# Cross attention on one core: scores of token tiles 2 and 3 issued together in the third block of a quarter

## What is computed

```python
x = x + xattn(layernorm(x), ctx, ctx, Wq, bq, Wk, bk, Wv, bv, Wo, bo)
# x is (2, 2048, 512), ctx is (2, 154, 512), 16 heads of 32
scores = einsum('bhqd,bhkd->bhqk', q, k) / sqrt(32)
attn = softmax(scores); out = einsum('bhqk,bhkd->bhqd', attn, v) @ Wo.T + bo
x = x + ffn(layernorm(x))
```

## Time and profile before

| what | value |
| --- | --- |
| median of 3 runs (range) | 3585.88 us (3585.81 to 3586.5) |
| the profiled execution: its own time, its span | 3587.36 us, 3585.6 us |
| PE, DVE, ACT, POOL busy, share of the span | 96%, 63%, 42%, 32% |
| mean granted clock of PE | 0.987 |

### The profile page before, as it was taken

One profiled execution on the slowest core, in us unless ns is written; L12 is line 12 of the kernel. 1 busy time (PEld: TensorE's weight loads), 2 busy tenths in 40 slices (PEclk: granted clock), 3 DMA queues, 4 the chain that ended last, 5 costly groups with the idle time before them and its releaser, 6 DMA issues. The chain is left out here.

```text
span 3585.6 us, 56360 instructions
## 1 busy us (share of the span) xinstructions
PE 3447.5 (96%) x20560; PEld 2795.2 (78%) x20560; DVE 2271.9 (63%) x4996; ACT 1500.6 (42%) x3978; POOL 1138.8 (32%) x1008
## 2 busy tenths in 40 slices
PE   7999996999999989999999989999999899999999
PEld 5676675888888877888888868888888678888887
DVE  6888875999999984222322259999999642333322
ACT  5666663555555543111111145555555421111111
POOL 3434433555555520000000045555555121101111
PEclk9999998999999999999999989999999999999999
DMA  4112213111121122111111121112111331111111
GB/s 123 42 45 64 71 42 124 57 55 58 61 68 60 57 73 88 44 44 43 42 43 44 64 75 57 57 55 75 57 59 53 97 111 40 46 49 49 40 41 38
DMA packets 186869, 216.26 MB, mean 60 GB/s; under 512 B 27094, under 2 KB 125654, under 8 KB 186595
## 3 DMA queue, kind: packets, MB, share of 16 engines
q1 hardware_dynamic: 186595, 212.65, 18.5%
HBM read 125.79 MB, written 69.00 MB: 54 GB/s over the span
## 5 line engine op out<-in xcount | busy, mean ns | idle before, releaser
L1893 DVE SCALAR_TENSOR_TENSOR u_full<-banks,b_cols,gate 128x512 f32<-128x512 f32 (+1 forms) x176 | 132.1, 751 | 875.4 <-ACT gate L1851 802.4
L46 PE MATMUL banks<-fxT_h,w_h 128*128 128x512 f32 (+1 forms) x1408 | 556.3, 395 | 3.0 <-DVE w_l L1877 2.6
L48 PE MATMUL banks<-fxT_h,w_l 128*128 128x512 f32 (+1 forms) x1408 | 556.1, 395 | 0.0
L47 PE MATMUL banks<-fxT_l,w_h 128*128 128x512 f32 (+1 forms) x1408 | 555.2, 394 | 0.0
L1851 ACT ACTIVATE gate<-banks,b_cols 128x512 f32<-128x512 f32 (+1 forms) x176 | 121.2, 689 | 1007.1 <-PE banks L48 1007.1
L1746 POOL TENSOR_TENSOR sums<-sums,b_rows 128x512 f32<-128x512 f32 x64 | 85.2, 1363 | 877.6 <-DMA sums<-z_rows 877.6
L1146 POOL TENSOR_TENSOR rn<-ssq,neg_half 128x8 f32<-128x8 f32 x128 | 210.8, 1647 | 412.3 <-DVE ssq L1419 405.9
L46 PE MATMUL banks<-wqkv_h,hT_h 128*128 128x512 f32 x768 | 324.9, 423 | 15.0 <-DVE wqkv_l L1406 15.0
L1355 ACT ACTIVATE pT_h<-banks 128x384 fp32r<-128x384 f32 (+2 forms) x512 | 213.9, 470 | 257.5 <-PE banks L1244 256.5
L1460 DVE TENSOR_SCALAR prob<-prob,rc 128x384 f32<-128x384 f32 (+2 forms) x512 | 313.5, 654 | 9.1
L46 PEld LDWEIGHTS banks<-fxT_h,w_h 128*128 128x128 f32 (+1 forms) x1408 | 259.6, 184 | 72.0 <-DVE w_l L1877 4.3
(11 more groups left out here) (190 smaller groups left out, 8183.2 us busy)
## 6 DMA issues: line engine op xcount, KB each, us to landing
y_rows<-sums SPq DMA_DIRECT2D x16, 1024.0 KB
sums<-y_rows SPq DMA_DIRECT2D x64, 256.0 KB, 3.0
z_rows<-sums SPq DMA_DIRECT2D x64, 256.0 KB, 2.0
sums<-z_rows SPq DMA_DIRECT2D x16, 1024.0 KB, 5.8
thirds<-in_w SPq DMA_DIRECT2D x30, 512.0 KB, 4.8
thirds<-in_x SPq DMA_DIRECT2D x8, 1024.0 KB, 6.8
x_rows<-thirds SPq DMA_DIRECT2D x8, 1024.0 KB, 4.3
thirds<-y_rows SPq DMA_DIRECT2D x64, 128.0 KB, 2.8
```

What stands on the lines that cost most here:

```text
L46: pe.matmul(out, a_h, b_h, start=start, stop=False)
L47: pe.matmul(out, a_h, b_l, start=False, stop=False)
L48: return pe.matmul(out, a_l, b_h, start=False, stop=stop)
L1893: e.scalar_tensor_tensor(out=u_full[r, m % 2, :], in0=ps[r, 2 * (m % 2), :], scalar=b1[r, place[m], 0:1], in1=gate[r, :], op0=ALU.add, op1 ...
```

## The change

Nothing is computed otherwise. In the 31 quarters in which scores of a next quarter are made:

- PE: `scores` of tile 2 leaves block 1 and stands in block 2, directly in front of `scores` of tile 3.
- ACT: `exps` of tile 2 goes from block 1 to block 2, and `exps` of tile 3 from block 2 to block 3, behind `hi_q` and `hi_p` of that block.
- DVE: `maxima` of tile 2 goes from block 1 to block 2. `maxima` of tile 3 stays in block 2 but goes behind `lo_p`. `recip` of tiles 2 and 3 goes from blocks 2 and 3 to blocks 3 and 4.
- POOL: its code is unchanged, but its divisions of tiles 2 and 3 wait for those reciprocals.

```diff
 PE
-                            if k < GT - 1 and not (g.last and q == DC - 1):
-                                scores(it, q + 1, k + 1)
+                            if k in (0, 2) and not (g.last and q == DC - 1):
+                                scores(it, q + 1, k + 1 if k == 0 else k)
+                                if k == 2:
+                                    scores(it, q + 1, 3)
                             transpose_p(it, m, g.last)
 ACT
-                            if k < GT - 1 and more:
-                                exps(it, q + 1, k + 1)
+                            if k in (0, 2, 3) and more:
+                                exps(it, q + 1, max(k, 1))
 DVE
-                            if k < GT - 1 and more:
-                                maxima(it, q + 1, k + 1)
+                            if k in (0, 2) and more:
+                                maxima(it, q + 1, max(k, 1))
                             if k == 1 and (q or old):
                                 lo_o(it, q - 1)
-                            if k < GT and more:
-                                recip(it, q + 1, k)
+                            if k in (0, 1, 3, 4) and more:
+                                recip(it, q + 1, (0, 1, None, 2, 3)[k])
                             lo_p(it, QK * q + k, 4 + (QK * q + k if g.last else turn(q, k, 0)) % 2)
                             if (q, k) in X_SLOT and not g.last:
                                 lo_x(it + 1, X_SLOT[q, k], 4 + turn(q, k, 1) % 2)
+                            if k == 2 and more:
+                                maxima(it, q + 1, 3)
```

## The result

The changed kernel took 3595.70 us (median of 11 runs, 3592.57 to 3599.87), the kernel before, run beside it, 3587.37 us (11 runs, 3585.81 to 3589.21). The ratio is 1.0023 with a 95% interval of 1.0014 to 1.0033: 8.3 us slower, where 9.1 had been forecast. That is clear of noise; whether it is more than the 0.2% (7.2 us) at which the prediction counts a change as one is not settled by this interval.

A forecast was written before the change was run, and what follows sets the result against it. Chains through ACT and DVE were taken to set the time around PE's waits, PE only the stretches between. Terms 11.3 - 4.5 + 0.65 + 1.65 = +9.1 us on 3585.9 gave 3595.0 us; range 3586 to 3602, including the cancelling case.

The forecast's parts named there:

- PE's drain, 0.3 us a pair: On PE, merging two groups of scores spares a tiling-mode drain, 0.3 us in each of 31 quarters.
- The list of PE's waits: Seven recurring PE waits per group before the change, four naming DVE, two ACT, one POOL, adding to 4.81 us.
- Quarter 2, +0.72: Exponents of tile 3 push `hi_p` of block 4 on ACT, so the next quarter's first `maxima` starts 0.72 us late.
- Quarter 3, +0.89: Exponents of tile 3 delay `hi_p` of block 4; the next `maxima` is 1.61 us late, 0.89 more than at quarter start.
- The hold of 1.25 us: In quarter 3 POOL's bias addition holds DVE's negative of the maxima, 1.25 us for some 0.17; forecast to meet tile 2.
- Quarter 0, nothing: DVE's chain to `lo_q` has no gap, so the 1.61 us lateness is carried unchanged to the projection.
- Quarter 1, -0.75: `lo_q` starts 0.76 us earlier and the transposes of block 4 leave 0.75 us earlier.
- both parts of it: Quarter 1: `hi_q` behind tile 2's exponents only, and two `finish` at 1.00 us for 1.53 without a division beside them.
- Sum: Middle group 0.72 + 0.89 - 0.75 = +0.86 us; whole phase 11.3 - 4.5 + 0.65 + 1.65 = +9.1 us.
- 1.61 - 0.3 + 1.95: 1.61: quarters 2 and 3 of a group; +1.95: last group's extra; 0.3: PE regains in that group's quarter 0.
- PE is the bound: Faster rival: PE bounds throughout, each merge saves its drain, -9.3 us in all, 3576.6; chance 0.13.
- Much slower by the stalls: Rival: late divisions stall PE in block 0 by 0.84 and 2.17 us, quarter 1 regains nothing; +21, 3607; chance 0.10.

The follow-up runs named there:

- the one-quarter runs: Four kernels, each with the new order in only one of quarters 0, 1, 2, 3: periods 64.88, 64.09, 65.63, 65.88 us against 64.90 in the kernel before.
- the quarter alone: New order only in quarter 2, old order in the others: period 65.63 us against 64.90 in the kernel before.
- quarter 0 alone: New order only in quarter 0, old order in the others: period 64.88 us against 64.90 in the kernel before.
- The kernel with the exponents back in front: Changed kernel with exponents of tile 3 back in block 2, directly behind those of tile 2: period 68.26 us against 65.74.
- quarter 3 alone: New order only in quarter 3, old order in the others: period 65.88 us against 64.90 in the kernel before, groups with clock falls left out.
- short division: Changed kernel, last division of quarters 2 and 3 cut to one head of four: 65.76 us in one stretch without clock falls, later 68.1 to 68.2.
- quarter 1 alone with the moved additions: New order only in quarter 1, POOL's bias additions moved: to quarters 1 and 2, 3586.49 us; all behind quarter 0, 3581.92 us; which one is not said.

## Why the prediction was right, step by step

- *PE's drain, 0.3 us a pair:* the scores together do run closer, but the one-quarter runs show no gain from it in quarters 0, 2 and 3, and the gain of quarter 1 has another source. In quarter 0 it ended as idle time. The list of PE's waits in the prediction was one short: the wait of 0.36 for exponents in quarter 0 (311.49) is missing, so there were eight and 5.17 us of them. It changed no term, since that time too went into the wait for the queries.
- *Quarter 2, +0.72:* measured 0.72 on DVE, 0.71 on PE, and 0.73 for the quarter alone. The forecast of two waits at unchanged ends held (1.10 and 0.82, forecast 1.3 and 0.8), as did the wait for POOL in block 0 of quarter 3, 0.78, and the single wait for exponents, 1.10 for 1.3.
- *Quarter 3, +0.89:* measured 0.95 to 0.98. The hold of 1.25 us was where I had put it; taking it away is worth 0.66 us a group (65.74 - 65.08). The transposes of quarter 0 started 2.06 late, where I had 2.17, but PE's wait for POOL in front of them was 1.01 and not over 2: PE itself came 1.3 late to it (314.10 - 1.01 - 2.97 = 310.12, before 309.07 - 0.25 = 308.82), which I had not followed.
- *Quarter 0, nothing:* the projection came 1.67 late for 1.61, and quarter 0 alone gave -0.02.
- *Quarter 1, -0.75:* measured -0.83, and -0.81 alone. `finish` at 1.00 and the wait of 0.62 (forecast 0.7) show that both parts of it came. They cannot be priced apart. In the kernel before `hi_q` (the row below, timeline of ACT before) ended at 342.47 and the two `finish` at 342.36, and `lo_q` followed at 342.50. By these rows an earlier `hi_q` alone would have given some 0.2 us at most and a shorter `finish` alone nothing; that is an estimate. The kernel with the exponents back in front had the short `finish` (1.00) with a `hi_q` that was later still; there `lo_q` waited 1.32 for `hi_q`, and the quarter gained nothing.

```profile
341.77 0.70 ACT L759 ACTIVATE xqT_h<-banks,bq_cols 128x512 fp32r<-128x512 f32 x1
```

- *Sum:* +0.84 a group for +0.86, and +8.3 between the medians for +9.1. In the traces the phase itself is 8.91 longer, but part of that closeness is luck, since two misses cancel. Up to block 4 of quarter 1 in the first group the loss is 0.53, where I had +0.65, with one fall of the clock in it (73 to 77 us) that the kernel before does not have. From the same row in the seventh group to the end of the phase it is 2.6, where my terms give 1.61 - 0.3 + 1.95 = 3.3. The six periods between add to 5.75 and not to the 5.16 forecast, since three of them are longer than 65.76 (66.04, 65.90 and 65.97), two of these by a fall of the clock, for which the prediction had no term. The chances do not add up as written either: with a quarter of 0.55 below 7.2 us they come to 0.51, 0.36 and 0.13 and not to 0.53, 0.32 and 0.15.
- *The rivals:* "PE is the bound" is out by the one-quarter runs. "Much slower by the stalls" is not what the changed kernel does, but its mechanism appears as soon as the divisions get another 0.9 us later.

## What to carry to other kernels

When work is moved one block later in an in-order queue, what it costs is decided by the next instruction behind it, and who waits for that: here four exponents of 1.46 us were free in one quarter, won 0.8 in another where they had stood in front of something urgent (and a division moved out of the way with them), and lost 0.7 and 1.0 where they came to stand in front of the high part of block 4. A pattern that repeats need not have one answer for all its repeats, so such a change should be tried for each of them alone. And a merge that closes gaps on the fullest engine gives nothing if the time is set by a chain through the others; look at which wait ends last.

## What the runs showed of the hardware that I had not expected

PE's granted clock fell behind some of its longer waits. In the changed kernel (windows of PE: busy us, granted clock, DMA), behind a wait of 1.01 us that ended at 182.46:

```profile
178.00:182.00 4.00, 3.14 (x22) 1.00 0.00 0
182.00:186.00 4.00, 3.54 (x11) 0.57 0.01 4
186.00:190.00 4.00, 4.00 (x27) 1.00 0.00 0
```

The transposes there took 1.09 us for four in place of 0.66, and matmuls of 512 columns 0.63 in place of 0.39, for some 3 us. Behind the equal wait at 314.10 nothing of the kind happened. The kernel before has no such fall between 90 and 545 us; its waits there reach 1.18. Between the same times the changed kernel has two in its profiled execution, quarter 0 alone has one and quarter 3 alone four, three of these behind waits of 1.17 and 1.18 that the kernel before has too. The kernels with waits of 1.43 (exponents back) and 1.27 with 1.90 (short division) have one in every group and, from the third group on, two in every group. So the length of the wait in front does not settle it, and what does no run here shows. One fall costs PE 1.4 to 1.6 us: from the transposes at 182.46 to those two blocks later it is 7.84, and 6.28 behind 314.10. How much of it reaches the end of the group depends on where it comes: 0.16 in the changed kernel (a period of 65.90 in place of 65.74), where the wait for the queries in front of the projection took up the rest, and all of 1.4 with quarter 3 alone (67.26 for 65.88), where it came in quarter 2. This fits the wider scatter of the changed kernel, 7.3 us from the fastest to the slowest run for 3.4 of the kernel before, and over its 11 runs the slowest has a mean granted clock of 0.984 and the two fastest 0.987. But quarter 1 alone with the moved additions scatters by 7.9 us, also with the lower clocks (0.984 and 0.985) in its slowest runs, while its trace has no fall between 90 and 545 us. A trace exists only of one run of each, so falls of this kind as the cause of the scatter are argued, not shown.

The holds were the other point. An instruction of four columns on DVE, 0.17 us when nothing is in its way, took 1.25 us beside an addition on POOL (303.40 before, 306.91 changed) and another one 1.14 (344.92), each until the addition was over. The Trainium skill (SBUF — State Buffer, SBUF: two separate sides) states that a VectorE instruction in a 2-port mode and a GpSimd instruction take the port pair that they share in turn, and whichever starts first keeps it for its whole instruction. The two holds agree with it; that so small an instruction pays for all that is left of the other engine's was new to me.
